# Moving small operations between and within the engine queues of a three-block transformer kernel

## What is computed

```
ada = silu(c) @ W_ada + b_ada              # shift, scale, gate for attention and for the MLP
h   = layernorm(x) * (1 + scale_a) + shift_a
x   = x + gate_a * (attention(h) @ W_proj + b_proj)
h   = layernorm(x) * (1 + scale_m) + shift_m
x   = x + gate_m * (gelu(h @ W_fc1 + b_fc1) @ W_fc2 + b_fc2)     # 1152 hidden channels
```

## Time and profile before

| what | value |
| --- | --- |
| times of three executions | 2201.18, 2196.90, 2199.78 us |
| median | 2199.78 us |
| the profiled execution | 2201.18 us, its span 2199.5 us |
| granted TensorE clock, mean over the span | 0.956 of full speed |
| busy time of PE, DVE, ACT, POOL | 2017.1, 1255.3, 1108.5, 1034.2 us |

### The profile page before, as it was taken

How to read it: one execution, slowest core, us unless ns; L and a number is a source line. 1 busy time by engine, 2 the same in 40 slices (tenths; PEclk the granted TensorE clock), 3 DMA queues, 4 the chain that set the end, 5 groups by cost and what they waited for, 6 DMA issues and landing times. The chain is left out here.

```text
span 2199.5 us, 50545 instructions
## 1 busy us (share of the span) xinstructions
PE 2017.1 (92%) x16725; PEld 1778.2 (81%) x16725; DVE 1255.3 (57%) x3034; ACT 1108.5 (50%) x1911; POOL 1034.2 (47%) x1056
## 2 busy tenths in 40 slices
PE   6697378999999998979999999998989999999996
PEld 2465267999999897869899998987878989898986
DVE  7487545555646566456555565656565646565541
ACT  2121145556565655545655646465456565656552
POOL 0200335555555454466455455544665545454544
PEclk9986689999999999999999999999999999999998
DMA  7402334333333333343333333333343332333320
GB/s 202 111 4 87 92 86 133 90 97 96 87 102 87 95 84 101 101 111 98 102 91 95 98 86 102 85 97 98 85 118 102 85 97 83 107 85 103 90 77 25
DMA packets 138576, 207.62 MB, mean 94 GB/s; under 512 B 34702, under 2 KB 94958, under 8 KB 138190
## 3 DMA queue, kind: packets, MB, share of 16 engines
q1 hardware_dynamic: 110478, 163.48, 27.0%
q10 hardware_dynamic: 24192, 27.94, 4.5%
q0 software_dynamic: 3808, 14.96, 2.4%
HBM read 99.74 MB, written 20.82 MB: 55 GB/s over the span
## 5 line engine op out<-in xcount | busy, mean ns | idle before, releaser
L1693 DVE TENSOR_REDUCE maxima<-scores 128x4 f32<-128x1024 f32 x384 | 461.2, 1224 | 187.7 <-PE scores L1448 182.9
L1510 PE MATMUL mlp_ps<-h_mlp,w_up 128*128 128x256 f32 (+1 forms) x3024 | 409.9, 288 | 31.0 <-ACT hidden L1268 19.9
L1024 POOL TENSOR_TENSOR hidden<-g_full,hidden 128x512 fp32r<-128x512 f32 (+1 forms) x240 | 282.3, 1186 | 325.5 <-ACT hidden L1268 324.7
L1510 PEld LDWEIGHTS mlp_ps<-h_mlp,w_up 128*128 128x128 f32 (+1 forms) x3024 | 378.4, 192 | 69.0 <-ACT hidden L1268 27.4
L1225 ACT ACTIVATE probs<-scores 128x1024 f32<-128x1024 f32 x384 | 383.7, 1028 | 73.9 <-PE pv_ps L1485 45.6
L1365 PE MATMUL mlp_ps<-w_down,hidden 128*128 128x288 f32 x2592 | 392.1, 296 | 0.0
L1365 PEld LDWEIGHTS mlp_ps<-w_down,hidden 128*128 128x128 f32 x2592 | 373.4, 190 | 18.8
L1448 PE MATMUL scores<-k_stack,q_stack 108*128 108x512 f32 x768 | 244.6, 411 | 34.7 <-DVE maxima L1693 21.7
L1471 PE MATMUL scores<-q_stack,k_stack 110*128 110x256 f32 x1536 | 245.2, 292 | 7.0 <-DMA q_stack<-neg_max 3.8
L1471 PEld LDWEIGHTS scores<-q_stack,k_stack 110*128 110x128 f32 x1536 | 206.1, 189 | 36.6 <-issue 19.8
L1215 ACT ACTIVATE neg_max<-att_ps 16x256 fp32r<-16x256 f32 x48 | 18.0, 375 | 428.3 <-PE att_ps L1458 428.3
(11 more groups left out here) (191 smaller groups left out, 3017.5 us busy)
## 6 DMA issues: line engine op xcount, KB each, us to landing
q_stack<-qk SPq DMA_DIRECT2D x144, 180.0 KB
k_stack<-qk SPq DMA_DIRECT2D x288, 90.0 KB
inv_sum<-inv_scratch ACTq DMA_DIRECT2D x192, 128.0 KB, 2.6
k_stack<-qk SPq DMA_DIRECT2D x288, 54.0 KB
x_in<-out_x SPq DMA_DIRECT2D x48, 288.0 KB, 3.9
x_mid<-out_x SPq DMA_DIRECT2D x48, 288.0 KB, 4.2
out_x<-x_out SPq DMA_DIRECT2D x48, 288.0 KB, 3.1
q_stack<-qk SPq DMA_DIRECT2D x144, 72.0 KB
```

What stands on the lines that cost most here:

```text
L1024: tt(out, full, high.bitcast(F32), ALU.subtract).then_inc(signal, 1)
L1510: last = mm(up_bank[n % 2][:, (m % 2) * T:(m % 2 + 1) * T], w[:, m * P:(m + 1) * P], h, start=count == 0, stop=count == 6)
L1693: nc.vector.tensor_reduce(out=maxima[:, :, :, u], in_=scores[u % 2][:, :, :, :], axis=AX.X, op=ALU.max).then_inc(s_max, 1)
```

## The change

Five edits, all of them in the order or the place of work:

1. The stack's low part of h_att is made by DVE (`attention_stack`), not by POOL: twice in DVE's prologue, and in each half-step ahead of the maximum of unit 6. POOL's `attention_low` keeps only the low part h_att[1], and its waits for `s_h_a` and for its own results go.
2. POOL's `add_mlp` does both token tiles, behind `attention_low` (and in b = B - 2 behind the staging of weights). Before, the first tile was done ahead of `attention_low`.
3. ACT's `v_evict(it + 1, 0)` stands behind `gather_sums`, and in b = 1 also behind the last conversion of w_up.
4. TensorE's `score_unit(it + 1, 0)` stands behind `up(m, 4)`, not ahead of it.
5. The epilogue calls the new `add_mlp`.

```diff
--- before.py
+++ after.py
@@ -1057,14 +1057,8 @@
                         stage(l + 1, n % SLOTS)
 
             def attention_low(it):
-                pool.wait_ge(s_h_a, NCH * it + NCH)
                 pool.wait_ge(s_hhi_a, NCH * it + NCH)
                 low(h_att[1][:, :, :], h_full[:, 0:2, :], h_att[0][:, 0:2, :], s_hlo_a)
-
-                rows = slice(C - 2 * P, 2 * (C - 2 * P))
-                pool.wait_ge(s_hlo_a, it + 1)
-                low(h_att[0][rows, 2, :], h_full[rows, 2, :], h_att[0][rows, 2, :], s_hst_a)
-                pool.wait_ge(s_hst_a, it + 1)
 
             def prologue():
                 for n in range(SLOTS):
@@ -1106,14 +1100,12 @@
                 for half in range(2):
                     pool.wait_ge(s_o_norm, 2 * it + half + 1)
                     low(o_att[1][:, half, :], o_full[:, half, :], o_att[0][:, half, :], s_o_lo)
-                if before:
-                    add_mlp(it - 1, 0)
                 if after_next:
                     attention_low(it + 2)
                 if at(b, B - 2) and after_next:
                     stage_behind(l + 1, OF["w_in"])
                 if before:
-                    add_mlp(it - 1, 1)
+                    add_mlp(it - 1)
 
             def add_attention(it):
                 pool.wait_ge(s_xmid, 16 * it + 16)
@@ -1133,11 +1125,13 @@
                 low(hidden[1][:, tiles, :].rearrange("p a t -> p (a t)"), g_full[:, n % 2, 0:width],
                     hidden[0][:, tiles, :].rearrange("p a t -> p (a t)"), s_g_lo)
 
-            def add_mlp(it, t):
-                pool.wait_ge(s_down_gated, 2 * it + t + 1 + PRE2)
-                if t == 0:
-                    pool.wait_ge(s_x_st, 16 * it + 16 * B)
-                tt(x_out[:, t, :], x_one[:, t, :], gated[:, t, :], ALU.add).then_inc(s_x_out, 1)
+            def add_mlp(it):
+                for t in range(2):
+                    pool.wait_ge(s_down_gated, 2 * it + t + 1 + PRE2)
+                    if t == 0:
+
+                        pool.wait_ge(s_x_st, 16 * it + 16 * B)
+                    tt(x_out[:, t, :], x_one[:, t, :], gated[:, t, :], ALU.add).then_inc(s_x_out, 1)
 
             def epilogue():
                 it = L * B - 1
@@ -1146,8 +1140,7 @@
                 mlp_low(it)
                 for n in range(UP_USES):
                     hidden_low(it, n)
-                for t in range(2):
-                    add_mlp(it, t)
+                add_mlp(it)
 
             whole_run(pool, prologue, half_step, epilogue)
 
@@ -1307,11 +1300,11 @@
                 if before:
                     load_table(ACT.Gelu_apprx_tanh)
                 copy_o(it, 1)
-                if after:
-                    v_evict(it + 1, 0)
                 gather_sums(it)
                 if at(b, 1):
                     high_weights("w_up", l, (5,))
+                if after:
+                    v_evict(it + 1, 0)
                 if before:
                     gelu(it - 1, 0)
                 load_sums(it)
@@ -1583,12 +1576,9 @@
                     for n in range(2, UP_USES):
                         if at(b, 1) and n == 2:
                             weights_ready("w_up", l)
-                        if after and n == UP_USES - 1:
-                            score_unit(it + 1, 0)
                         up(m, n)
-                elif after:
+                if after:
                     score_unit(it + 1, 0)
-                if after:
                     score_unit(it + 1, 1)
                 if after_next:
                     attention_transposes(it + 2)
@@ -1664,6 +1654,14 @@
                 tt(h[low_rows, 2, :], h_full[low_rows, 2, :], h[low_rows, 2, :].bitcast(F32), ALU.subtract)\
                     .then_inc(done, 1)
 
+            def attention_stack(it):
+
+                low_rows = slice(C - 2 * P, 2 * (C - 2 * P))
+                dve.wait_ge(s_h_a, NCH * it + NCH)
+                dve.wait_ge(s_hhi_a, NCH * it + NCH)
+                tt(h_att[0][low_rows, 2, :], h_full[low_rows, 2, :], h_att[0][low_rows, 2, :].bitcast(F32), ALU.subtract)\
+                    .then_inc(s_hst_a, 1)
+
             def qk_low(it, n):
                 dve.wait_ge(s_qk_hi, QK_USES * it + n + 1)
                 tiles = slice(2 * n, min(2 * n + 2, QK_TILES))
@@ -1745,6 +1743,7 @@
                 x_hats(0, 0, x_in, s_xhat_a)
 
                 convert_weights(0, OF["w_in"])
+                attention_stack(0)
                 dve.wait_ge(s_init, 5)
                 dve.wait_ge(s_kinit, 1)
                 last_rows = slice(P - 32, P)
@@ -1759,6 +1758,7 @@
                 attention_norm(1)
                 dve.wait_ge(s_tr_a, TRS)
                 x_hats(0, 1, x_in, s_xhat_a)
+                attention_stack(1)
                 for u in range(8):
                     unit_max(0, u)
 
@@ -1801,6 +1801,8 @@
                         normalise(it)
                     if u == 5 and before:
                         gate_down(it - 1, 0)
+                    if u == 6 and after_next:
+                        attention_stack(it + 2)
                     if after:
                         unit_max(it + 1, u)
                 if before:
```

## The result

The changed kernel takes 2225.56 us in the median of 4 executions (2221.36 to 2229.24), the kernel before 2198.34 us in the median of its 4 (2192.75 to 2201.18; the 2199.78 of the table above is that of the first three). The ratio is 1.0127, 95% interval 1.0097 to 1.0155: slower by 1.3%. The forecast was 2204.5 with a range from 2195 to 2212; the side was right, the size and its cause were not. The profiled execution took 2225.39 us, its span is 2223.7.

What follows compares the result with a forecast made beforehand. TensorE, busy 92% of the span, was taken to bound the kernel; +3.8 (eviction), +2.0 (score unit) and -1.1 (start) sum to +4.7 us, 2204.5 in terms of the median, range 2195 to 2212.

Steps and rivals of the forecast that it cites:

- The stack on DVE: DVE before unit 6 of the maxima: a subtraction of 0.42 us fits into 0.44 idle, costing nothing in the half-steps.
- the room of 0.68: Between DVE's last maximum and TensorE's transposes: 0.68 us by which the maxima could slip without cost.
- Rival D: DVE's stack waits for ACT's modulation and holds up the maxima: 0.42 us in 46 half-steps, +19, 2219 us; chance 0.04.
- The eviction: ACT, behind the gather: up(2) starts 0.23 us later, +0.05 or +0.18 a half-step after absorption, +3.8 us in all.
- the absorbing stall: TensorE at up(3), waiting for gelu(1) behind load_sums: 0.18 us a half-step, 0.05 in the last layer, absorbing up(2)'s delay.
- Rival A: load_sums' issue is pushed back, gelu(1) moves with gelu(0), nothing absorbed: 10.8 us over 43 half-steps, 2211.5 in all; chance 0.18.
- Rival B: The gather of the sums goes out 0.41 us earlier, gelu(1) no longer stalls up(3): -5.2 us, 2194.6; chance 0.13.
- The score unit: TensorE in b = 1: two score matmuls come after the wait for a GELU, 0.66 us three times, +2.0 us.
- The start: Before the loop: TensorE's first qk projection starts 0.73 to 1.1 us sooner as DVE takes POOL's second operation, -1.1 us.
- add_mlp: POOL, first addition behind attention_low: x_out's first half comes later but no TensorE wait moves; nothing, bounds -1 and +1.

Runs made afterwards that it cites:

- e2: The kernel before with only the stack's low part moved to DVE: 2220.16 us, ratio 1.0092 to the kernel before.
- e5: The changed kernel with the second operand of DVE's stack subtraction read from PSUM instead of SBUF: 2197.59 us, ratio 0.9991 to the kernel before.
- e3: The kernel before with only the eviction of the values moved behind the gather's issue: 2201.01 us, ratio 1.0009 to the kernel before.
- e9: The kernel before with only ACT's gelu(1) moved ahead of load_sums: 2190.38 us, ratio 0.9965 to the kernel before.
- e10: The changed kernel with DVE's stack subtraction behind the second gate multiplication and gelu(1) ahead of load_sums: 2196.58 us, ratio 0.9996 to the kernel before.
- e11: e10 with the eviction of the values back ahead of the gather's issue: 2188.05 us, ratio 0.9949 to the kernel before.
- e4: The kernel before with only score unit 0 moved behind up(4): 2201.95 us, ratio 1.0009 to the kernel before.
- e8: The kernel before with only both additions of the MLP result behind attention_low on POOL: 2198.78 us, ratio 0.9997 to the kernel before.
- e1: The changed kernel with only the stack's low part given back to POOL: 2202.46 us, ratio 1.0012 to the kernel before.

## Why the prediction was wrong, point by point

- **The stack on DVE, forecast to cost nothing: here it failed.** The step took its 0.42 us from L1664, an instruction of the same shape that starts just ahead of one of POOL's, and gave it to a place where POOL is already at work. The contention was to be seen in the kernel before, in POOL's row for h_mlp (1.28 us at the least, 1.52 in the median) and not in DVE's. The runs put 1.24 us at unit 6 (e2), 0.41 with one operand in PSUM (e5). The second mistake is the room of 0.68: it was counted from the last maximum's end to the transposes' start, but the transposes start 0.23 after the maximum that they wait for (1206.01 to 1206.24), so it was 0.45. The delay of 0.86 less 0.45 is the 0.41 measured; at 0.41 there is no loss, as e5 shows, so this mistake alone would have cost nothing. Rival D had the right place and the right chain, its price of 0.42 a half-step was 0.64, and its chance of 0.04 was far too small, since it looked for late data and not for a slow instruction.
- **The eviction, forecast +3.8 us.** Its mechanism held, to 0.01 us in the eviction's start; up(2) came 0.29 later and not 0.23. Measured 0 to +4 us alone (e3), with half-steps that grew by 0.02 and 0.07. The term was right in kind and rather too large: the absorbing stall was bigger than read, as e9 shows. Rival A fell in the kernel before. Its size came in e10 against e11 (8.5 us for the 10.8), but not by its mechanism: there the absorbing stall had been taken away, while in the changed kernel load_sums is issued 2.11 us behind the gather (1186.10 to 1188.21), no later than the 2.15 before. Rival B fell: the issue still starts 0.63 behind the copy's start.
- **The score unit, forecast +2.0.** Measured 0 to +4 (e4); its place in b = 1 remains argued.
- **The start, forecast -1.1.** TensorE's first projection starts 1.5 us earlier, by the trace, and 0.9 is left at the first transposes of the maxima.
- **add_mlp, forecast nothing.** Measured nothing (e8).

e1 measures all edits but the stack. The forecast gave them 3.8 + 2.0 = +5.8 us; measured are +2.7 (2202.46 against 2199.79), interval +0.9 to +4.6. To the stack the forecast gave -1.1; measured alone are +20.4 (e2), interval +17 to +23. The whole change was forecast at +4.7 and measured at +27.2, and the missing 22 us are the stack's.

## What to carry to other kernels

A duration belongs to the neighbours it was measured beside. So compare the least and the median duration of one instruction, on both engines: where they differ and no idle time stands in front, another engine may hold it up. Before an instruction is moved to an engine's idle time, look at what the other engines run then, above all POOL beside a DVE instruction with two operands in SBUF, and take the price from a row with the same neighbour. Room in front of a waiter is less than the time from the work's end to the waiter's start, by what the waiter needs to pick up the signal. A delay may be free only because another stall covers it; who removes that stall pays for the delay.

## What the runs showed of the hardware that was not expected

- An instruction that is held up by the other engine shows no idle time in front of it; its own duration grows, 0.41 to 1.24 us, and DVE's busy time with it.
- Which of the two is held up depends on which starts first: at unit 6 DVE's subtraction waited 0.83 us, behind the gate POOL's addition was stretched by 0.22 and DVE's stayed at 0.41. Either way the one held up goes on 0.14 us before the recorded end of the other.
- TensorE's transposes began 0.23 us after the end of the DVE instruction that they waited for (1206.01 to 1206.24), the projection behind them 0.05 after the end of another one (1206.50 to 1206.55). So it does not lie in DVE. Ahead of the transposes TensorE's queue has wait instructions of its own: the trace of the changed kernel shows those of its L1448 and L1449 at 1206.0 and 1206.1, after the maximum's end. That they take the rest of the 0.23 was not tested.
- ACT's sequencer issues a DMA of 0.35 us beside an activation that is already under way at next to no cost to it (e9: the activation beside it takes 0.62 us, 0.59 without); behind an issue of 0.53 with nothing under way the eviction started 0.19 after the issue's end and pushed gelu(0) back by 0.23.
